# Scaling a bias row as 16 rows of 128 values on VectorE and broadcasting the result, in a fused attention and feed-forward kernel

## What is computed

```python
x = x + attn(layernorm(x), ctx, ctx, q_norm_w, k_norm_w, w_out)
x = x + ffn(layernorm(x), ...)
# ffn
w_up = dequant4bit(w_up_q, w_up_scale).T
y1 = x1 @ w_up + b_up + x1 @ w_up_lora_a @ w_up_lora_b
x2 = relu(y1)
w_down = dequant4bit(w_down_q, w_down_scale).T
y2 = x2 @ w_down + b_down + x2 @ w_down_lora_a @ w_down_lora_b
```

## Time and profile before

| | before |
|---|---|
| median of 3 runs | 482.93 us |
| the profiled execution | 484.46 us |
| its span | 482.7 us |
| PE busy | 443.0 us, 92% |
| DVE busy | 352.0 us, 73% |
| ACT busy | 300.3 us, 62% |
| POOL busy | 282.1 us, 58% |
| mean granted TensorE clock | 0.979 |

### The profile page before, as it was taken

How to read it: one execution, slowest core, us unless ns; L and a number is a source line. 1 busy time by engine, 2 the same in 40 slices (tenths; PEclk the granted TensorE clock), 3 DMA queues, 4 the chain that set the end, 5 groups by cost and what they waited for, 6 DMA issues and landing times.

```text
span 482.7 us, 8285 instructions
## 1 busy us (share of the span) xinstructions
PE 443.0 (92%) x2416; PEld 218.2 (45%) x2416; DVE 352.0 (73%) x1076; ACT 300.3 (62%) x927; POOL 282.1 (58%) x304
## 2 busy tenths in 40 slices
PE   0285869999999999999999999999999999999997
PEld 0164545444444444444444444444444445444443
DVE  3899998979879786868686877778777856534341
ACT  1698978878858675757575757666675856422120
POOL 5477767685859574848384747576657745451100
PEclk9996879999999999999999999999999999999999
DMA  8679769789777858887867777897697777474422
GB/s 224 215 245 175 189 206 209 114 167 141 160 121 137 168 109 160 135 171 114 171 130 155 134 158 132 169 132 161 122 135 163 118 153 110 91 125 93 88 56 74
DMA packets 207740, 70.36 MB, mean 146 GB/s; under 512 B 196880, under 2 KB 200096, under 8 KB 207056
## 3 DMA queue, kind: packets, MB, share of 16 engines
q1 hardware_dynamic: 206864, 69.35, 72.7%
q10 hardware_dynamic: 752, 0.34, 0.3%
q0 software_dynamic: 80, 0.16, 0.2%
HBM read 17.15 MB, written 4.19 MB: 44 GB/s over the span
## 4 chain that ended last, share of the span: by engine, by line
PE 78%; DVE 1%; DMA 1%; SPq 0%; issue 0%
PE ff L951 33%; PE ff L937 33%; PE tb L919 8%; PE sb L891 2%; PE tb L907 2%; DMA x<-hid 1%; SPq L401 0%; PE tb L877 0%; DVE t_sin L1171 0%; DVE pr L1203 0%; DVE y L1253 0%; DVE stats L1184 0%; DVE x L1181 0%; DVE q L1212 0%; DVE q L1118 0%
## 5 line engine op out<-in xcount | busy, mean ns | idle before, releaser
L951 PE MATMUL ff<-wd_hi,x 128*128 128x512 f16 x512 | 152.3, 379 | 0.7 <-DMA x<-hid 0.7
L937 PE MATMUL ff<-wu_hi,xnT 128*128 128x512 f16 x512 | 152.7, 380 | 0.0
L691 ACT ACTIVATE pr<-pr,nmax 128x128 f32<-128x128 f32 x256 | 99.0, 389 | 13.6 <-DVE nmax L1203 12.9
L515 POOL TENSOR_TENSOR big<-pr,big 128x512 f16<-128x512 f32 x64 | 80.9, 1272 | 32.6 <-ACT big L722 32.6
L937 PE MATMUL ff<-wu_lo,xnT 128*128 128x512 f16 x256 | 97.0, 379 | 0.0
L951 PE MATMUL ff<-wd_lo,x 128*128 128x512 f16 x256 | 97.0, 379 | 0.0
L506 POOL TENSOR_TENSOR pr<-pr,rinv 128x512 f32<-128x512 f32 x64 | 72.7, 1137 | 35.6 <-DVE rinv L1111 35.6
L756 ACT ACTIVATE hid<-z 128x512 f16<-128x512 f32 x64 | 39.9, 624 | 80.1 <-DVE z L1132 80.1
L1203 DVE CUSTOM_DVE_ANT_0 pr<-sb,tabs,score_scale 128x128 f32<-128x128 f32 x256 | 73.8, 344 | 12.3 <-PE sb L891 11.2
L937 PEld LDWEIGHTS ff<-wu_hi,xnT 128*128 128x128 f16 x512 | 48.2, 98 | 58.4 <-issue 5.9
L1132 DVE SCALAR_TENSOR_TENSOR z<-ff,su,b_row 128x512 f32<-128x512 f32 x64 | 47.7, 745 | 36.0 <-PE ff L937 34.7
(11 more groups left out here) (144 smaller groups left out, 652.7 us busy)
## 6 DMA issues: line engine op xcount, KB each, us to landing
xt<-in_x SPq DMA_DIRECT2D x16, 256.0 KB, 3.0
big<-in_L_ffn_w_up_q SPq DMA_DIRECT2D x4, 1024.0 KB, 7.3
big<-in_L_ffn_w_down_q SPq DMA_DIRECT2D x4, 1024.0 KB, 6.2
out<-y SPq DMA_DIRECT2D x16, 256.0 KB, 2.7
wd_lo<-in_L_xattn_w_out SPq DMA_DIRECT2D x1, 1024.0 KB, 7.5
pT<-big SPq DMA_TRANSPOSE x64, 3.5
b_row<-in_L_ffn_b_up SPq DMA_DIRECT2D x1, 1024.0 KB, 9.1
x<-hid SPq DMA_TRANSPOSE x64, 3.2
```

What stands on the lines that cost most here:

```text
L515: pool.tensor_tensor(p3[:, m, :, 1, :], pr[:, m], p3[:, m, :, 0, :], ALU.subtract).then_inc(p_low, 1)
L691: last = act.activation(pr[:, m, g, :], pr[:, m, g, :], ACT.Exp, bias=nmax[:, p, j:j + 1], scale=-1.0, accum_out=rsum[:, p, j:j + 1])
L937: last = pe.matmul(bank[:], a[:, m, :], b[:, m, 512 * g:512 * g + 512], start=(m == 0 and i == 0), stop=(m == KC - 1 and i == 2))
L951: last = pe.matmul(ff[down_bank[n]][:], x2T[:, part, k + h % HG, :], b[:, h, :], start=(h == 0 and i == 0), stop=(h == HC - 1 and i == 2))
```

## The change

`bias_row` and its four operations on ACT are gone, with `BIAS_ROW_AT`. Instead DVE scales `b_flat` (16 by 128) once, in the chain of `find_scales`, into a corner of the buffer `z`. SP stores these 2048 values to a new tensor in memory, in slot 193 of the new numbering, which stands between the load of batch 1 and that of w_out. The load of `b_row` reads the new tensor and waits for that store. `hidden` waits once, for the load. The load of weight group 2, which overwrites `b_flat`, waits for the scaled copy.

```diff
+        b_scaled = z[0:HC, 0, 0:P]
+        b_store = nc.dram_tensor("bias_scaled_row", (H,), F32).ap()
@@ load_group
                 if g == 2:
                     sp.wait_ge(tops_ready, 7)
+                    sp.wait_ge(bias_scaled, 1)
@@ sync
+                if s == BIAS_STORE_AT:
+                    sp.wait_ge(bias_scaled, 1)
+                    sp.dma_start(b_store.rearrange("(p a) -> p a", p=HC), b_scaled).then_inc(bias_stored, 16)
                 if s == ROW_LOAD_AT:
-                    sp.dma_start(b_row[:], bu.rearrange("(a n) -> a n", a=1).broadcast_to([P, H])).then_inc(bias_row_in, 16)
+                    sp.wait_ge(bias_stored, 16)
+                    sp.dma_start(b_row[:], b_store.rearrange("(a n) -> a n", a=1).broadcast_to([P, H])).then_inc(bias_row_in, 16)
@@ scalar
-            def bias_row(g):
-                act.wait_ge(scale_steps, SCALE_STEPS)
-                act.wait_ge(bias_row_in, 16)
-                part = b_row[:, 512 * g:512 * g + 512]
-                act.activation(part, part, ACT.Identity, scale=kap[:, 5:6]).then_inc(bias_scaled, 1)
@@ find_scales
                 link(dve.tensor_scalar(kap[:, 5:6], kap[:, 4:5], X2_TOP, None, ALU.mult))
+                dve.tensor_scalar(b_scaled, b_flat, kap[0:HC, 5:6], None, ALU.mult).then_inc(bias_scaled, 1)
@@ hidden
-                        if n == 0:
-                            dve.wait_ge(bias_scaled, g + 1)
+                        if n == 0 and g == 0:
+                            dve.wait_ge(bias_row_in, 16)
@@ tables, two of about 60 lines
-R_VSUM = (476, 800, 1176, 1835)
+R_VSUM = (511, 875, 1251, 1910)
-R_QLOW = (18, 345, 975, 1516)
+R_QLOW = (93, 420, 1070, 1591)
```

More of the change, by code:

```diff
@@ L42 @@
[L42 to L46, removed]
@@ L55 @@
[L55 to L66, removed]
@@ L67 @@
[L67 to L73, removed]
+R_STATS = (0, 94, 482, 1441)
@@ new lines @@
+R_SQUARES = (87, 90, 636, 1640)
+R_MOMENTS = (6, 108, 558, 1475)
+R_KEYS = (0, 90, 378, 1946)
+R_POW = (87, 89, 844, 2021)
+R_CENTRE = (88, 134, 733, 1768)
+R_SINES = (87, 185, 624, 1564)
+R_COSINES = (88, 102, 746, 2138)
+R_ROPE = (88, 279, 768, 1576)
+R_KSPLIT = (89, 256, 1137, 1807)
+R_KLOW = (107, 286, 1090, 1571)
+R_KTURN = (499, 715, 1360, 1677)
+R_QSPLIT = (98, 345, 1067, 1845)
+R_QLOW = (93, 420, 1070, 1591)
+R_QTURN = (484, 712, 1356, 1694)
+R_SCORES = ((138, 584, 1448, 1915), (250, 603, 1558, 1935), (275, 703, 1698, 1955), (341, 909, 1737, 2010))
@@ new lines @@
+R_PLOW = ((490, 1135, 2139, 2502), (532, 1145, 2281, 2540), (593, 1499, 2393, 2682), (613, 1610, 2472, 2700))
+R_PTURN = ((762, 1383, 1826, 1997), (809, 1470, 1842, 2080), (1125, 1507, 1858, 2142), (1131, 1564, 1874, 2156))
+R_VSUM = (511, 875, 1251, 1910)
+R_VARG = (536, 661, 1175, 1802)
+R_VPOW = (611, 773, 1213, 2466)
+R_VSPLIT = (786, 1418, 1898, 2268)
+R_VLOW = (714, 1583, 2284, 2716)
+R_PV = (917, 1661, 2014, 2351)
+R_OHIGH = (893, 1602, 2122, 2421)
+R_OLOW = (733, 1485, 1870, 2195)
+R_PROJ = (1068, 1757, 2094, 2387)
@@ new lines @@
+R_X1 = (877, 1579, 2026, 2294)
+R_POW2 = (944, 2150, 2572, 2873)
+R_YBASE = (2137, 2695, 2892, 3119)
+R_XN = (1044, 1926, 2245, 2620)
+R_XNLOW = (1009, 1730, 2035, 2343)
+R_XNTURN = (1343, 1814, 2090, 2320)
+R_UP = ((1324, 1936, 2250, 2600), (1456, 1973, 2319, 2613), (1601, 2012, 2326, 2628), (1707, 2070, 2365, 2667))
+R_Z = ((1234, 1821, 2121, 2400), (1277, 1851, 2185, 2461), (1377, 1939, 2249, 2515), (1543, 1971, 2292, 2570))
+R_X2HIGH = ((1424, 2110, 2387, 2678), (1550, 2148, 2437, 2715), (1573, 2191, 2481, 2828), (1824, 2212, 2517, 2858))
@@ L75 @@
+R_X2LOW = ((1269, 1848, 2143, 2420), (1399, 1909, 2265, 2490), (1428, 1996, 2278, 2566), (1593, 2005, 2296, 2585))
+R_DOWN = ((1837, 2142, 2432, 2710), (1853, 2162, 2466, 2731), (1903, 2205, 2517, 2733), (1914, 2211, 2518, 2789))
+R_RESULT = (1801, 2129, 2479, 2730)
+R_STORE = (2203, 2425, 2748, 2971)
+R_LOAD = (1670, 1696, 2091, 2382)
+R_X2TURN = ((1630, 1942, 2234, 2476), (1638, 1969, 2254, 2503), (1675, 1990, 2280, 2542), (1695, 2079, 2291, 2543))
 UP_TILES, DOWN_TILES = 16, 16
@@ L86 @@
[L86 to L104, removed]
+DEQ_AT = (92, 96, 97, 121, 135, 160, 162, 163, 174, 325, 356, 215, 363, 374, 541, 557, 635, 717, 728, 832, 912, 884, 1016, 1025,
+          1088, 1136, 1147, 1182, 1273, 1750, 1424, 1906)
@@ new lines @@
+TURN_AT = (97, 104, 126, 196, 246, 260, 361, 394, 518, 568, 659, 731, 874, 884, 1062, 1065, 1156, 1163, 1164, 1202, 1274, 1311,
+           1399, 1425, 1527, 1536, 1616, 1649, 1730, 1775, 1813, 1882)
+HIGH_AT = (148, 161, 218, 274, 317, 399, 574, 650, 664, 720, 739, 832, 885, 887, 911, 974, 1013, 1034, 1070, 1076, 1199, 1222,
+           1345, 1402, 1474, 1556, 1611, 1767, 1772, 1890, 1892, 1966)
+REST_AT = (0, 0, 0, 282, 360, 0, 618, 665, 713, 0, 0, 0, 1224, 1258, 0, 0, 0, 0, 0, 0, 0, 0, 0, 0, 0, 0, 0, 0, 0, 0, 0, 0)
@@ new lines @@
+LOW_AT = (164, 165, 170, 301, 364, 517, 651, 743, 756, 612, 621, 699, 1092, 1331, 753, 861, 901, 956, 1055, 1061, 1139, 1168,
+          1236, 1255, 1306, 1315, 1474, 1547, 1557, 1683, 1754, 1757)
+LOAD_AT = (454, 506, 642, 659, 1177, 1254, 1362)
+WO_LOAD_AT = 328
+ROW_LOAD_AT, DOWN_BIAS_LOAD_AT = 1318, 902
+BATCH_LOAD_AT = (192, 625, 1583)
+LORA_BHIGH_AT, LORA_BLOW_AT = 92, 90
+LORA_B_ROWS_AT = (456, 819)
+LORA_TURN_AT = (87, 88, 89)
+LORA_COPY_AT = (101, 106, 251)
+WO_ORDER_AT = (130, 136, 137, 184)
@@ L105 @@
+WO_TURN_AT = (268, 297, 448, 459)
+WO_HIGH_AT = (334, 442, 478, 502)
+WO_LOW_AT = (440, 441, 479, 483)
+LORA_A_AT, LORA_ALOW_AT = (91, 93), (89, 91)
+LORA_D_LOAD_AT, NORM_SCALES_AT = 191, 5
+BIAS_STORE_AT = 193
+WO_SQUARES_AT, WO_SUM_AT, WO_ARG_AT, WO_POW_AT = 131, 90, 168, 172
 RING, W_RING, HID_RING = 4, 3, 3
```

36 lines of the change are left out of this document (6 added, 30 removed).

## The result

The changed kernel takes 485.5 us (median of 18 runs, 484.2 to 486.6), the kernel before 483.7 us (18 runs on the same chips). The ratio is 1.0035, with a 95% interval of 1.0023 to 1.0046: slower by 1.7 us (1.1 to 2.2). The forecast was no change, +0.8 us, in a range that ended at 485.2. Of the distance of 1.8 us between 485.5 and the forecast of 483.7, 0.75 us lie in the base: the three runs shown ahead had a median of 482.93, the 18 later ones 483.68. The other 1.0 us lies in the terms of the sum.

The account below looks back on a forecast made before the run. DVE was taken to bound the ramp from 20 to 104 us, then PE for 375.00 us. Terms 0.2 + 1.25 - 0.65 = +0.8 us on 482.93 gave 483.7 us, range for 8 in 10 from 482.2 to 485.2.

Parts of the forecast that it names:

- ACT's four operations: ACT, 69.2 to 81.6 us: removing 2.8 us of operations gives nothing, since DVE is the bound there; 0.
- The row's load: Load issued at 58.2 us, first needed by DVE at 75.67: hidden by 8 us; 0.
- One operation on DVE: DVE behind 13.94 us: one more scaling in a chain of small steps, nothing hides it; +0.2 us, bounds 0.1 and 0.33.
- SP's wait: SP at the start: w_out and weight group 1 issued 4.6 us later, still in time for ACT and DVE; 0.
- The rival of 485.5 us through SP: SP's wait reaches ACT through w_out landing past 22.6 us: up to 1.8 us slower, 485.5; chance 0.06.
- ACT's copy ahead of the squares: ACT's first w_out copy delays squares and PE's first turns by about half a microsecond, absorbed later; 0, bound +0.4.
- The sum of squares: PE, sum ahead of tile 8: PE waits from about 43.0 to 45.0 us, DVE loses a turn; +1.25, bounds 0.3 and 2.2.
- The low part of q: DVE near 69 us, behind two weight low parts: PE's turn comes earlier, DVE's waits shrink; -0.65 us, bounds 0 and -0.68.
- The clock's rival: PE stays longer at the lower clock past about 53.5 us: about 1.0 us slower, 484.7; chance 0.27.
- The sign of being wrong: Forecast wrong if PE's unbroken run starts before 104 or after 105.5 us, or PE has idle time after it.

Follow-up runs that it names:

- the store late: The changed kernel with the store of the scaled row issued after w_out and weight groups 1 and 2; 1.0032 to the kernel before, +1.5 us.
- both moves back: The changed kernel with PE's sum of squares of batch 0 and DVE's low part of q of batch 2 back in place; 1.0000 to the kernel before.
- two pairs of runs: Sum of squares moved back in the changed kernel: 1.0013; it alone moved, on the kernel before with the bias change: 1.0022; ratios to the kernel before.
- The kernel with memsets: Kernel before plus bias change, q's low part behind two weight low parts, three POOL operations replaced by constant writes; 1.0014 to the kernel before, +0.7 us.
- q alone moved: Kernel before with the bias change and one move, batch 2's low part of q behind two weight low parts on DVE; 1.0015, +0.7 us.
- the four kernels: Weight group 7's load ahead of k's transpose: q alone moved 1.0127, the old order 1.0054, changed kernel 1.0143, the kernel with memsets 1.0104, to the kernel before.
- the old order: The kernel before with the bias change alone, its order kept in every queue, the store ahead of w_out; 0.9999 to the kernel before, 0.0 us.

## Why the prediction was wrong

By its own steps:

- **ACT's four operations, 0**: right. The bias change alone gives 0.0 us, give or take 0.8, though ACT is 2.8 us lighter.
- **The row's load, 0**: right; no wait for it shows anywhere.
- **One operation on DVE, +0.2**: 0.21 us in the trace. At the end it is less than the runs can tell (0.0, give or take 0.8).
- **SP's wait, 0**: right. With the store late the time is the same within its interval, and w_out landed 2.5 us ahead of its use. The rival of 485.5 us through SP met the measured time by chance, not by its mechanism.
- **ACT's copy ahead of the squares, 0**: right at the end (both moves back: 0.0 us), though the ramp near 41 us is 0.3 us later in the trace. Executions differ there by as much: the bias change alone, without this move, is 0.2 us later too (40.45 against 40.22 for the same low part of w_out, and 40.51 in the changed kernel).
- **The sum of squares, +1.25**: right at its place and nearly in size. Measured 1.06 and 1.1 us by two pairs of runs, each give or take 0.75. I had written that what PE loses, DVE loses. That holds up to 53 us; the way from there to the end stands in no trace, and the changed kernel's profile had lost most of the delay by 66 us. So that the size fits so well may be luck in part.
- **The low part of q, -0.65**: this step failed, in its sign. It costs 0.6 to 0.8 us. I wrote "That one now comes 0.67 us earlier (69.39 less 68.72), and PE with it", which happened, and took DVE's own operations as fixed in length. They are not: at the new place they meet POOL's reads and give away 1.26 us. The same mistake is in "its idle 2.9 us (84.00 less 81.10) are all that a change of order there could give back": DVE's busy time has waits for POOL in it, such as the 1.65 us for an operation of 0.69. I also wrote that "The transposed q of batch 2 is later by about 1.2 us, but is used only after 76 us", and did not follow what stands behind it in SP's queue: k's transpose, weight group 7 and the four transposes of probabilities, all about 2 us later. My bounds of 0 and -0.68 left out a loss without a reason for it. The error of the sum, 1.0 us, is 0.65 + 0.7, less what the sum's term and DVE's operation were too large by.
- **The clock's rival**: not borne out. From 41 to 52 us the mean granted clock was 0.50 before and 0.62 in the changed kernel, so it rose earlier there, not later, though PE had been idle 1.28 us longer ahead of the sum; from 52 to 60 us it was 1.00. Two kernels with the same order on PE, before and with the bias change alone, stand at 0.50 and 0.81 in 41 to 52 us, further apart than these two. With one profile each that is all the rows can say.
- **The sign of being wrong**: I had named a start of PE's unbroken run before 104 or after 105.5 us. It was 104.37, so by the profile alone the forecast would have passed. The runs decide, since one profile can lie a microsecond off the median.

What stays open is how q's 0.7 us divides between the longer DVE operations and the later queue. The kernel with memsets shows that the queue alone can hold DVE back at 81 us. In the changed kernel's one profile DVE had made up most of the loss by 96 us; in that of q alone moved it had not. The rows show each mechanism, not its share at the end. Open too is how the sum's delay gets from 53 us to the end.

## What to carry over

Before an operation is moved on one engine, look at what POOL does at the new place: a DVE operation with two inputs in SBUF is only as short as POOL's reads let it be, and rows of two lengths for the same form (here 0.68 and 1.1 us) are the sign. DVE's busy time is then no floor, since waits for POOL are inside it. Follow a moved operation's output through the queue that issues its transfer, with all that stands behind it there, transposes and weight loads too. A wait put on PE in a chain without slack cost most of its length here (1.1 us by the runs, of 1.28 us more idle time ahead of the sum), however light another engine had become.

## What was not expected of the hardware

- The DMA transpose of k landed 2.8 us after its issue in the changed kernel and 4.1 us in the kernel before, where it went ahead of a load of 1 MB, and 6.3 to 6.9 us in the four kernels in which it was issued behind that load on the same queue. That change of order cost 2.6 us on the old order and 5.2 us on the changed one (1.0143 less 1.0035).
- A DVE operation of 0.68 us took 1.09 to 1.65 while POOL read SBUF, and another of 0.74 us took up to 1.46. Beside POOL operations that only write, the same two took 0.68 and 0.74. Which engine was first by 0.05 us decided over 0.86 us of DVE's time near 60 us.
- The time of one and the same kernel spreads over 3 us (482.5 to 485.65 in the 18 runs of before), which is more than the effect. One profile can lie a microsecond off the median on either side: the kernel before was profiled in an execution of 484.46 us with a median of 483.68, the bias change alone in one with a span of 481.0, 1.7 us shorter than that one, though their medians agree. So a change of this size is sized by runs and explained by traces.
